# A windowed-attention kernel with copies of transposed probabilities one or two slots later, their products two slots later, four buffers for them, and the work around them laid out anew

## The reference, cut to what matters

```python
h = concat([clip(sum_abs_diffs(image), 0, 1),            # (16, 256, 256): two 2x2 differences, absolute values added
            table[x_txt]], axis=1)                       # (16, 77, 256)  -> h is (16, 333, 256)
n = layernorm(h)
q, k, v = heads(n @ Wq + bq), heads(n @ Wk + bk), heads(n @ Wv + bv)      # 16 heads of 16
for each of 5 windows of 128 rows (starts 0, 64, 128, 192, 205):
    out[window] += softmax(q k^T / 4 + pos_bias[head]) @ v                # per head, then divided by the overlap count
h = h + merged @ Wo + bo
r = layernorm(h)
scores, experts = top2(softmax(r @ gate))                # 8 experts
h = h + sum over the two experts of score * (silu(r @ w1[e]) * (r @ w3[e])) @ w2[e]
```

## Time and profile before

| | |
|---|---|
| time, median of 3 runs | 1400.3 us (1399.01 to 1402.45) |
| the profiled execution | 1394.69 us, of it 1392.9 us from the first to the last instruction |
| busy share PE, DVE, ACT, POOL | 85%, 66%, 56%, 44% |
| granted TensorE clock, mean | 0.919 |
| stage one (attention and all around it) | from the start to some 866 us |
| stage two (91 expert tiles) | some 872 us to the end |
| DMA | 123.36 MB, mean 89 GB/s |

### The profile page before, as it was taken

How to read it: one execution, slowest core, us unless ns; L and a number is a source line. 1 busy time by engine, 2 the same in 40 slices (tenths; PEclk the granted TensorE clock), 3 DMA queues, 4 the chain that set the end, 5 groups by cost and what they waited for, 6 DMA issues and landing times.

```text
span 1392.9 us, 35049 instructions
## 1 busy us (share of the span) xinstructions
PE 1189.1 (85%) x10190; PEld 951.8 (68%) x10191; DVE 920.9 (66%) x4211; ACT 782.9 (56%) x3176; POOL 611.8 (44%) x900
## 2 busy tenths in 40 slices
PE   2386888988988998888889872999999999999996
PEld 1254656655655665555556551999999999999995
DVE  4485989888888889898997864344444444444442
ACT  0196998989899998899899980211111111111110
POOL 5333466565646655665665334122322232232232
PEclk9698899889898988999998985899999999999998
DMA  3694563465357446634643507232233323323222
GB/s 110 133 234 100 109 132 89 95 131 113 88 103 142 92 92 116 128 89 94 133 107 71 96 24 234 36 50 46 49 47 48 49 45 49 48 46 48 46 49 31
DMA packets 98402, 123.36 MB, mean 89 GB/s; under 512 B 15544, under 2 KB 87416, under 8 KB 95192
## 3 DMA queue, kind: packets, MB, share of 16 engines
q1 hardware_dynamic: 75880, 89.96, 30.6%
q0 software_dynamic: 18576, 24.47, 10.9%
q10 hardware_dynamic: 3808, 7.34, 1.8%
HBM read 69.35 MB, written 46.07 MB: 83 GB/s over the span
## 4 chain that ended last, share of the span: by engine, by line
PE 47%; POOL 16%; issue 14%; DMA 12%; ACT 4%; SPq 3%; DVE 3%; POOLq 0%; DVEq 0%; ACTq 0%
PE s_bank L1168 12%; PE t_bank L1168 12%; PE o_bank L1183 11%; DMA qk_parts<-parts_flat 5%; POOL expert_slots L493 4%; DMA expert_slots<-rows,slot_i 4%; DMA stacks<-qk_parts 3%; PE m_bank L1104 3%; ACT probs L622 3%; PE t_bank L1040 2%; SPq L372 2%; POOL rest L502 2%; PE o_bank L1063 2%; POOL parts_flat L507 2%; PE m_bank L1157 1%
## 5 line engine op out<-in xcount | busy, mean ns | idle before, releaser
L622 ACT ACTIVATE probs<-probs,neg_max 128x128 f32<-128x128 f32 x1280 | 497.4, 401 | 21.6 <-DVE neg_max L757 21.0
L757 DVE CUSTOM_DVE_ANT_0 probs<-s_bank,nbias 128x128 f32<-128x128 f32 x1280 | 293.0, 284 | 38.4 <-PE s_bank L1026 36.9
L622 ACT ACTIVATION_READ_ACCUMULATOR probs<-probs,neg_max 128x1 f32 x1280 | 257.4, 201 | 0.0
L1040 PE MATMUL t_bank<-ident,probs 128*128 128x128 f32 x1280 | 221.0, 300 | 28.7 <-ACT probs L622 26.7
L681 ACT ACTIVATE v_all<-s_bank 128x512 f32<-128x512 f32 x91 | 54.4, 598 | 286.9 <-PE s_bank L1168 286.9
L1026 PE MATMUL s_bank<-stacks 96*128 96x128 bf16 x1280 | 136.5, 233 | 68.8 <-DMA stacks<-qk_parts 46.9
L1026 PEld LDWEIGHTS s_bank<-stacks 96*128 96x128 bf16 x1280 | 93.4, 105 | 132.4 <-DMA stacks<-qk_parts 50.7
L1040 PEld LDWEIGHTS t_bank<-ident,probs 128*128 128x128 f32 x1280 | 150.1, 153 | 45.7 <-ACT probs L622 41.7
L636 ACT ACTIVATE probsT<-t_bank 128x512 f32<-128x512 f32 x240 | 141.9, 591 | 57.5 <-PE t_bank L1040 56.7
L1183 PE MATMUL o_bank<-stacks,v_all 128*128 x728 | 172.6, 380 | 0.7 <-issue 0.5
L597 POOL DMA_INDIRECT out_dram<-wq_sb,nbias x46 | 75.7, 1645 | 198.5 <-DVE wq_sb L967 185.3
(11 more groups left out here) (158 smaller groups left out, 2079.4 us busy)
## 6 DMA issues: line engine op xcount, KB each, us to landing
stacks<-qk_parts SPq DMA_DIRECT2D x192, 166.5 KB, 5.6
qk_parts<-parts_flat SPq DMA_DIRECT2D x192, 83.2 KB
nbias<-expert_slots SPq DMA_DIRECT2D x91, 129.0 KB, 2.0
w_sb<-in_L_ffn_w_dram ACTq DMA_DIRECT2D x14, 512.0 KB, 5.2
v_all<-v_all SPq DMA_DIRECT2D x64, 96.0 KB, 6.4
x_here<-in_x_dram SPq DMA_DIRECT2D x16, 256.0 KB, 5.7
out_dram<-h_res SPq DMA_DIRECT2D x16, 256.0 KB
stacks<-in_L_ffn_w_dram SPq DMA_DIRECT2D x8, 512.0 KB, 8.5
```

The costliest lines, as they stand in the source:

```text
L622: ins = act.activation(seg, seg, ACT.Exp, bias=neg_max[:, r, i:i + 1], scale=-1.0, accum_out=row_sum[:, (par + v) % 2, h:h + 1])
L757: ins = dve.tensor_tensor_reduce(probs[:, r, i * WIN:(i + 1) * WIN], s_bank[:, k % 2, i * WIN:(i + 1) * WIN], nbias[:, h, :], 1.0, BIG, AL ...
L1040: mm = pe.transpose(t_bank[:, (k - 3) % 2, i * WIN:(i + 1) * WIN], probs[:, r, i * WIN:(i + 1) * WIN], ident[:, :])
```

## The change

It shifts the tail of each group's path, gives it more buffers, and moves almost every piece of extra work to another slot.

```diff
-        probsT = sb("probsT", [P, 2, GH * WIN])
+        probsT2 = sb("probsT", [P, 2, GH * WIN])
+        probsT = [probsT2[:, i, :] for i in range(2)] + [w3_sb[:, E - 2, c, :] for c in range(C)]
 # SP
                     load_stack(0, q_stack[par1], Q_SLOTS)
                     write_part(1, 2, part3_ready)
-                    if tail:
-                        store_h2()
-                    load_stack(1, k_stack[par1], K_SLOTS)
                     vt = v_win[par1]
                     sp.wait_ge(v_ready, b1 * 3 + 3)
...
                     sp.dma_start(vt[64:128, 3, :], vt[o:o + 64, 4, :]).then_inc(v_shift_in, 16)
+                    load_stack(1, k_stack[par1], K_SLOTS)
+                    if tail:
+                        store_h2()
...
+            sp.wait_ge(pv_done, B * G)
+            sp.dma_start(w3_sb[:, E - 2], w3[E - 2].rearrange("(c p) n -> p c n", p=P)).then_inc(expert_weights_in, 16)
 # ACT: the copy stands ahead of the exponentials of its slot, one slot later
+                    g = (k - 3) % NG
+                    if g != 3 and ((k >= 3 and att) or (k < 3 and tail)):
+                        n = b * G + (k - 3)
+                        act.wait_ge(pT_done, n + 1)
+                        if n >= 4:
+                            act.wait_ge(pv_done, n - 3)
+                        act.activation(probsT[n % 4], t_bank[:, n % 2, :], ACT.Copy).then_inc(pT_by_act, 1)
...
-                    v = (k - 4) // NG
-                    if (k - 4) % NG == 3 and ((att and v >= 0) or (tail and v < 0)):
+                    v = (k - 8) // NG
+                    if (k - 8) % NG == 0 and ((att and v >= 0) or (tail and v < 0)):
                         act.wait_ge(weightT_done, b * NW + v + 1)
 # DVE: its copy two slots later, ahead of the bias and maximum of its slot
+                    v = (k - 7) // NG
+                    if (k - 7) % NG == 0 and ((att and v >= 0) or (tail and v < 0)):
+                        n, wv, vp = b * G + (k - 4), b * NW + v, (par + v) % 2
+                        dve.wait_ge(pT_done, n + 1)
+                        if n >= 4:
+                            dve.wait_ge(pv_done, n - 3)
+                        dve.tensor_copy(probsT[n % 4], t_bank[:, n % 2, :]).then_inc(pT_by_dve, 1)
...
-                    if proj and k == 4:
+                    if proj and k == 5:
                         part_high(0)
-                    if proj and k == 6:
+                    if proj and k == 7:
                         part_high(1)
+                    if proj and k == 8:
                         part_middle(0)
...
-                    if proj and k == 8:
+                    if proj and k == 10:
                         part_middle(1)
 # PE: the product with v two slots later
-                    if (k >= 4 and att) or (k < 4 and tail):
+                    if (k >= 6 and att) or (k < 6 and tail):
-                        m, n = k - 4, b * G + (k - 4)
+                        m, n = k - 6, b * G + (k - 6)
```

More of the change, by code:

```diff
@@ L521, in step @@
                                            ALU.add).then_inc(ctx_added, 1)
-                    if inp and k == 0:
-                        pool.wait_ge(idx_in, b2 * 16 + 16)
+                    if att and k == 4:
+                        if b >= 2:
+                            pool.wait_ge(wo_done, b * 2 - 2)
+                        pool.memset(ctxT[par][:, :, :], 0.0).then_inc(ctx_zero, 1)
+                    if inp and k == 5:
+                        pool.wait_ge(conv_step, b2 * 3 + 2)
+                        pool.tensor_tensor(diag[:, :, :], diag[:, :, :], anti[:, :, :], ALU.add).then_inc(conv_step, 1)
+                        pool.wait_ge(conv_step, b2 * 3 + 3)
                         if b2 >= 2:
@@ L786, in step @@
                     if tail2 and k == 0:
+                        dve.wait_ge(logits_done, b9 + 1)
+                        dve.tensor_copy(logits[:, :, :], o_bank[:, 1 - par, 0:NT * E].rearrange("p (j e) -> p j e", j=NT))\
+                            .then_inc(logits_read, 1)
+                        dve.wait_ge(logits_read, b9 + 1)
+                        for j in range(NT):
+                            dve.max(best[:, j, :], logits[:, j, :]).then_inc(best_ready, 1)
+                        for j in range(NT):
+                            dve.wait_ge(best_ready, b9 * 6 + 1 + j)
+                            dve.max_index(best_i[:, j, :], best[:, j, :], logits[:, j, :]).then_inc(best_ready, 1)
+                    if tail2 and k == 1:
                         if b9 >= 1:
@@ L806, in step @@
                             .then_inc(taken_ready, 1)
-                    if tail2 and k == 2:
+                    if tail2 and k == 6:
                         dve.wait_ge(score_e_ready, b9 + 1)
@@ L822, in step @@
                         dve.wait_ge(token_step, b9 + 1)
-                    if tail2 and k == 3:
+                    if tail2 and k == 5:
                         counted = o_bank[:, par, 0:(NT + 1) * E]
@@ L895, in step @@
                         moments_of(h_in[par], stats1, moments1, b2, ln1_step)
[L896 removed]
+                    if inp and k == 16:
                         dve.wait_ge(rstd1_ready, b2 + 1)
@@ L900, in step @@
                         normalise(h_in[par], moments1, rstd1, lambda j: xn[:, j, :], xn_ready)
-                    if tail and k == 19:
-                        dve.wait_ge(logits_done, b0 + 1)
-                        dve.tensor_copy(logits[:, :, :], o_bank[:, par, 0:NT * E].rearrange("p (j e) -> p j e", j=NT))\
-                            .then_inc(logits_read, 1)
-                        dve.wait_ge(logits_read, b0 + 1)
-                        for j in range(NT):
-                            dve.max(best[:, j, :], logits[:, j, :]).then_inc(best_ready, 1)
-                        for j in range(NT):
-                            dve.wait_ge(best_ready, b0 * 6 + 1 + j)
-                            dve.max_index(best_i[:, j, :], best[:, j, :], logits[:, j, :]).then_inc(best_ready, 1)
             run_steps(step)
@@ L1083, in step @@
                         mm.then_inc(xT_done, 1)
-                    if tail2 and k == 2:
+                    if tail2 and k == 4:
                         counted = o_bank[:, par, :]
```

200 lines of the change are left out of this document (88 added, 112 removed).

## The result

The changed kernel takes 1461.6 us (median of 4 runs, 1454.6 to 1463.4; one more on record took 1466.4) where the kernel before takes 1400.1 beside it: a ratio of 1.0436, with a 95% interval of 1.0397 to 1.0475. The profiled execution has a span of 1452.9 us and a mean granted clock of 0.901 (before 1392.9 and 0.919). The prediction was 1447.

What follows compares the result with a forecast made beforehand. The prediction took a ring from S(0) over the cast and the k stack's landing as the limit. Per ring 0.6 + 2.1 + 0.6 = 3.3 us, 46 us over 14 rings, plus 1 at the ends: 1447 us, range 1404 to 1478.

Steps and rivals of the forecast that it cites:

- The limit: Whole step: a ring from S(0) over projections, parts and k stack to the next S(0) sets its length, 48.04 us.
- The cast, +2.1: Slots 8 to 10: M(8) to the end of part_middle(1) takes 6.2 us instead of 4.14; range +1.7 to +2.9 per ring.
- the first term: Start of a step, +0.6 us per ring; PE's slot 0 takes 4.93 us instead of 4.53.
- The start, +0.6: Slots 0 and 1: S(8) 1.2 us later at the lower clock, 1.4 earlier at full; +0.6 taken, range -1.4 to +1.2.
- Slots 2 to 7, 0: Slots 2 to 7: later copies and four buffers take nothing off ACT or PE, where neither waits; taken as 0.
- SP and the DMAs, +0.6: Cast to landed stack: more scatters fall there, three more give 1.3 us; +0.6 taken, range -0.5 to +2.0 per ring.
- Other moves, "worth nothing while the ring is the limit": After the cast and before S(0): xn normalised in slot 16, sum and clip on POOL; priced at nothing.
- The ends, +1: First two images and the last step, outside the 14 rings: 0 to 3 us added, say 1.
- Full clock at the start: Rival at the step start: -1.4 instead of +0.6 us, kernel 1419 us; chance 0.12.
- The ring opens: Rival: stack lands before PE wants it, ACT sets the step, 2.4 us less per step, kernel 1366 us; chance 0.10.

Runs made afterwards that it cites:

- Run 2: The changed kernel with the casts and splits of q and k put back to their old slots: 1409.0 us, ratio 1.0078 to the kernel before.
- run 1: The kernel before with only the cast part_middle(1) two slots later on DVE and split_last(1) one later on POOL: 1404.7 us, ratio 1.0060.
- run 3: The changed kernel with only ACT's copy of the transposed weights (WT) one slot later: 1457.9 us, ratio 1.0452 to the kernel before.
- run 5: The changed kernel with only PE's gate products moved from slot 0 to slot 19 of the step before: 1420.3 us, ratio 1.0177 to the kernel before.
- Run 10: The changed kernel with gate products and parts undone, and PV products (WT with them) one slot later than in the kernel before instead of two: 1392.3 us, ratio 0.9952.
- run 4: The changed kernel with SP's order as before (output rows, k stack, then the v shift): 1458.6 us, ratio 1.0441 to the kernel before.
- run 7: The kernel before with POOL's scatters moved from between the splits, split_last(1) behind split_rest(1), and part_middle(1) first behind M(8): 1390.1 us, ratio 0.9949.
- run 6: The kernel before with only the input's moments, reciprocal root and normalisation xn one to two slots earlier: 1375.9 us, ratio 0.9834.
- run 9: The changed kernel with gate products in slot 19 of the step before and casts and splits in their old slots: 1389.8 us, ratio 0.9941 to the kernel before.

## Why the prediction was right, and where it was off

**The limit.** A ring from S(0) over the projections, parts and stack to the next S(0): right. All 14 starts between 100 and 800 us wait for the stack, the cast ends at 29.3 us (28 to 29.5 foreseen), the steps are 51.7 us (some 51), the start is at the lower clock, E(0) is 1.9 us later (1.5).

**The cast, +2.1.** Measured +2.5, in the range of 1.7 to 2.9; the row of instructions in slots 8 to 10 is the one that was added up, and its 6.2 us were 6.13. The piece before the change is 3.59 as a mean, not the 4.14 of the one step I used, which makes up the difference. Run 2 shows that this part carries most of the loss. That its price hangs on the start, I had not seen: run 1 makes the same +2.5 cost 0.6 per step. The prediction added the terms as if they were free of each other. Here that is right, though not for a reason that it gives: the early xn takes PV's wait from the start, which the first term had counted (its 4.53 us of the kernel before hold the 1.29), and with it goes what would have paid the late cast back. In the kernel before the same sum would have been wrong.

**The start, +0.6.** Mis-sized: S(8) came 1.6 us later, M(8) 1.1, close to the upper end of 1.2 that was given for the lower clock. Choosing a value between the two clocks was the mistake; not one of the 14 starts ran at the full clock throughout, and nine were at 0.50 or 0.51. That M(8) meets the 1.2 is partly luck. PE's row alone gives 0.9 - 0.3 = 0.6 there; the 1.2 seems to be ACT's 1.5 - 0.3, and ACT isn't on the path (run 3). The 0.9 for S(2) was right (1.0), and another 0.6 arose in slots 2 to 7. The price inside it is the gate products', 2.2 us per step; without them S(8) would be 0.6 earlier than before (20.56 in run 5 against 21.14), by the other moves together. The part of the argument on ACT, with WT ahead of E(0), described a wait that is there and costs nothing (run 3).

**Slots 2 to 7, 0.** S(2) to S(8) is 0.6 us longer, and M(8) follows S(8) 0.55 sooner: together 0, by two things that cancel and that the prediction didn't have. Run 10 speaks for it in the time, as far as the second slot of distance goes.

**SP and the DMAs, +0.6.** The two pieces give 12.95 + 9.43 - 12.36 - 9.78 = +0.24. Of this kind of term it is near nothing, and run 4 finds SP's order free. The prediction had four or five of the six scatters behind the cast instead of two; in the trace three are issued behind it in nearly every step, and a fourth directly ahead of it. What they cost stays open. With the parts early, four scatters behind the cast (run 2, 13.37 + 9.44 = 22.81) and two (run 7, 13.18 + 9.65 = 22.83) take the same; with the cast late, none behind it (run 1, 12.21 + 9.65 = 21.86) is 0.5 less than three (the changed kernel, 22.38). These kernels differ in more than the scatters. The Trainium skill (DMA: Bandwidth & Descriptors, Queues, rings and completion order) gives a round robin between queues as the rule for sharing a DMA engine. By it I had put the term at the full 1.3; the runs show no such sum, and don't test the rule itself, since no run alters the scatters alone.

**Other moves, "worth nothing while the ring is the limit".** This sentence failed. Normalising xn earlier is ahead of S(0), but what it leaves behind S(0) when late is in the ring: PV waits for the logits' copy, which DVE reaches behind xn. Alone it is worth 23 us (run 6). In the changed kernel it is part of what the start gives back, and the gate products hid it. The wait of 1.29 us stood in the earlier trace rows and in the prediction's first step, so the sum had its end; I did not come back to it where the move that ends it was priced at nothing.

**The ends, +1.** Measured 1.3 for step 0, 3.2 for step 15, which has no stack to wait for behind it, and 2.0 behind the last score product. In step 15 the start is at the lower clock with the gate products in it: S(2) comes after 6.67 us instead of 3.65. By S(8) that is down to 1.3 (18.28 against 16.95), and at the last score product it is 3.2 again. How the 3.2 splits was not tried.

In sum 46 us were foreseen for the 14 rings and 53.3 measured (0.5 more per step for the start, 0.4 for the cast, 0.4 less for the DMAs), and 1 against 6.5 at the ends. That is 13 us of the 15 by which the forecast was low; the rest is that the medians lie 61.4 us apart and the profiled spans 60.0, and rounding.

**The rivals.** Full clock at the start: not here, but run 6 shows that it can be had, with an early xn. The ring opens: not by the change; in run 9 it does, with the cast at 23.4 us, and at a step of 47.0 us, not the 45.6 (48.05 - 2.4) of that rival. How much of run 6's gain is the clock and how much PV's wait is only argued: its six steps that start at the lower clock have S(2) at 4.4 to 5.2 us, against 6.0 as the mean before, and the other eight at 2.9 to 3.4. An estimate from these: the four at 0.50 throughout have 5.15, so the wait is worth some 0.9 of the 2.2 us by which S(2) comes earlier, and the clock 1.3.

## What to carry to other kernels

When a transfer closes a loop, cut the loop into pieces and read them as means over many rounds; then ask whether the engine that waits for the transfer waits again soon after, for something that does not need the transfer. While it does (here 1.1 us per step), a delay of the transfer is paid back, and a wait of 72 us costs 8. Once that second wait is gone, by whatever move, a delay costs nearly its full length. Work put directly behind the first wait costs its full length too. Work that needs nothing from the transfer belongs ahead of the wait: here twelve small products moved across it were 36 us.

## What the runs showed of the hardware

The granted clock of a step start doesn't go by the wait ahead of it alone: it was at half with a wait of 3.75 us and of 2.58 us, but also with no wait directly ahead in run 9 (four score products in 0.59 us at 498.17, straight behind the gate products), and at full behind a wait of 1.54 us in run 6. In run 9 PE had waited 1.13 us for ACT ahead of the gate products, and the clock was 0.76 as a mean over them, so it fell while they ran. Nor did it come back at once when PE had work: in the step of the changed kernel shown above PE was busy for 9.36 of 9.36 us at 0.50. The twelve gate products took 2.32 us at the lower clock (479.79 in the changed kernel), where the trace of run 6 has 1.33 us for them at a step's end with the clock up: 1.7 times as long, and not twice. The transposes of xn, from 0.80 to 1.37, are 1.7 times as long as well.
